# A subtraction of each normalized row tile, moved from VectorE to GpSimd, in the stage that finishes a graph attention layer

## The chip, the cores and the metric

The kernel runs on one core of a Trainium2 chip. The core's engines are TensorE (PE; its weight loads are PEld), VectorE (DVE), ScalarE (ACT), GpSimd (POOL) and SyncE (SP), each with an instruction queue of its own; they meet through semaphores. The metric is the device time of one execution in microseconds (us), lower is better. Before the change three timed runs gave 4061.72, 4068.97 and 4071.57 us, median 4068.97 us.

## What is computed

A graph network on 3125 nodes with 1024 features and 50000 edges: a layer norm and relu, a graph attention layer (GAT, 4 heads of 256), a residual sum, a second layer norm and relu, and two SAGE layers with a last residual sum. Cut to what matters here:

```python
h = jnp.maximum(_layernorm(x, axis=-1), 0.0)
x = x + relu(segment_sum(xp[src] * alpha[:, :, None], dst) + bias)   # attention layer, xp = h @ W
h = jnp.maximum(_layernorm(x, axis=-1), 0.0)
x = x + sage(relu(sage(h, W_self0, W_neigh0, b0)), W_self1, W_neigh1, b1)
```

`_layernorm` is `(x - mean) / sqrt(var + 1e-5)` along the row. The stage that the change touches begins when the sums over the edges are in SBUF and makes the second and third of these lines, up to the normalized h.

## The kernel before

The kernel is a sequence of stages with a barrier between them: tables of edges, a first normalization, the product with the attention weights, the sum over edges of the attention layer (`aggregate("gagg", ...)`), the finish of that layer (`gat_finish`, lines 1590 to 1716), and then twice a sum over edges and a product for the SAGE layers. All SAGE matmuls use f16 pairs: a row value v, scaled up, is kept as a high part, v rounded to f16, and a low part, v minus the high part, again in f16. A row of `h_rows` in DRAM is 1024 high parts, 1024 low parts and one scale.

`gat_finish` goes through 25 tiles of 125 rows by 1024 columns, with two slots for each buffer (slot = tile number modulo 2). For tile m:

- SyncE (`load`, L1621 to L1624) loads x and xp of the tile, in four DMAs, once x1 of tile m - 2 is ready.
- VectorE (`values`) computes four pieces of 256 columns at L1668 (own term plus edge sum), four at L1673 (division and bias), the relu and residual at L1676 (this gives x1, semaphore x1_ready at L1677), the row statistics at L1679 and L1682, and at L1683 the variance plus epsilon.
- ScalarE takes the root (L1704).
- VectorE (`normalize`) inverts it (L1690) and makes the shift (L1691).
- ScalarE computes the normalized, clipped row twice (L1713): h_sb in f32 and the first half of h16 in f16; then it counts up h_ready.
- VectorE (`split`, L1697) subtracts the f16 half from the f32 row and writes the result, in f16, to the second half of h16; it counts up lo_done.
- GpSimd stores x1 (`store_x1`, L1632) when x1_ready says so and h16 (`store_h`, L1636) when lo_done says so.

The order on each engine is written by `each_tile` (L136 to L152): straight code for tiles 0 and 1, then a loop of 11 turns with two tiles each, then straight code for the last ones. In its steady part it runs, on each engine, the `ahead1` step of tile m and then the `last` step of tile m - 1. So VectorE's order is values(m), normalize(m), split(m - 1), and GpSimd's is store_x1(m), store_h(m - 1). In the prologue values(0), normalize(0), values(1), normalize(1) follow each other with no split between; tile 2 is the first of the loop, and each even tile from 4 to 22 comes behind the loop's back edge. Tile 24 and the last two `last` steps come behind the loop. Inside the loop the tile number is a register, so that addresses of tile m and the values waited for are computed by the engine's queue ahead of the instruction that needs them; line 119 is the wait of the helper `chain`, by which VectorE waits for its own results.

Backward dependences: ScalarE writes h_sb and h16 of tile m only when lo_done covers tile m - 2 and the h store of tile m - 2 has landed; VectorE writes val of tile m only when the x1 store of tile m - 2 has landed and h_ready covers tile m - 2.

## Time and profile before

| | us |
|---|---|
| median of the three timed runs | 4068.97 |
| lowest, highest | 4061.72, 4071.57 |
| the profiled execution, own time | 4053.89 |
| its span, first to last instruction | 4052.2 |

The page of the profile gives busy time and share of the span by engine, and the span in 40 slices of 101 us, each digit a busy share in tenths. PEclk is the granted TensorE clock, in tenths of full speed; GB/s is what the DMA engines moved.

```profile
PE 3058.3 (75%) x20638; PEld 1746.6 (43%) x20638; DVE 2648.9 (65%) x4534; ACT 1150.8 (28%) x2637; POOL 1657.4 (41%) x1788
PE   0567878388888882007999999699668999997899
DVE  5646878688888887866555555555466555656443
POOL 4002222366666662114555555400145555555000
PEclk9978999699999996558999999899889999999999
```

The stage in question is slices 16 to 18 (counted from 1), where the PE row falls to 2, 0, 0. The profile numbers busy time only; register, branch and semaphore instructions of a queue are not in it, but can be asked for by line.

### The profile page before, as it was taken

How to read it: one execution, taken by the hardware profiler on the slowest of the kernel's cores; microseconds unless marked ns; L12 is line 12 of the kernel's file. 1: busy time of each engine (PE TensorE's matmuls, PEld its weight loads, DVE VectorE, ACT ScalarE, POOL GpSimd, SP SyncE). 2: the span in 40 equal slices, each digit the busy share in tenths (PEclk: the TensorE clock that was granted, in tenths of full speed). 3: DMA queues.
4: the chain of work that ended last, by engine and by line, in shares of the span. 5: the costliest groups of instructions: out<-in, count | busy, mean ns of one | idle time of the engine just before them, and what ended most of it. 6: DMA issues, size and time to landing. Idle time of an engine off the chain costs nothing. (4 is left out here: it accounts for less than half of the span.)

```text
span 4052.2 us, 74821 instructions
## 1 busy us (share of the span) xinstructions
PE 3058.3 (75%) x20638; PEld 1746.6 (43%) x20638; DVE 2648.9 (65%) x4534; ACT 1150.8 (28%) x2637; POOL 1657.4 (41%) x1788
## 2 busy tenths in 40 slices
PE   0567878388888882007999999699668999997899
PEld 0334544277777772003444444244324444442444
DVE  5646878688888887866555555555466555656443
ACT  3542343377777673310000000033200000000211
POOL 4002222366666662114555555400145555555000
PEclk9978999699999996558999999899889999999999
DMA  1456895388888885776999999622479999997333
GB/s 67 148 179 231 292 335 188 110 275 267 265 274 272 260 274 179 234 239 224 314 299 300 313 307 296 220 91 91 139 225 315 307 313 309 324 320 260 118 91 85
DMA packets 289524, 947.22 MB, mean 234 GB/s; under 512 B 57746, under 2 KB 58746, under 8 KB 289440
## 3 DMA queue, kind: packets, MB, share of 16 engines
q0 software_dynamic: 224912, 726.88, 53.8%
q1 hardware_dynamic: 64528, 219.29, 17.5%
q8 instruction: 45, 0.74, 0.1%
q14 instruction: 39, 0.32, 0.0%
HBM read 905.65 MB, written 130.59 MB: 256 GB/s over the span
## 5 line engine op out<-in xcount | busy, mean ns | idle before, releaser
L1434 POOL DMA_INDIRECT agg_got<-h_rows,agg_idx_now x896 | 898.0, 1002 | 654.3 <-issue 371.0
L1571 PE MATMUL agg_sum_ps<-agg_got,agg_hot 128*128 128x512 f16 x3584 | 878.1, 388 | 205.3 <-DVE agg_hot L1464 172.3
L1492 DVE TENSOR_TENSOR sum_acc<-agg_sum_ps,sum_acc 125x1024 f32 x448 | 548.7, 1225 | 434.4 <-PE agg_sum_ps L1571 322.9
L1555 PE MATMUL gagg_sum_ps<-gagg_got,gagg_hot_hi 128*128 128x256 f16 x3584 | 603.9, 274 | 198.6 <-DVE sums_acc L1492 129.3
L1571 PEld LDWEIGHTS agg_sum_ps<-agg_got,agg_hot 128*128 128x128 bf16 x3584 | 343.3, 99 | 664.0 <-DVE agg_hot L1464 216.9
L1530 ACT ACTIVATE gagg_hot_hi<-gagg_hot,gat_high_e 128x128 f16<-128x128 f16 x1792 | 547.7, 388 | 277.5 <-DVE gagg_hot L1459 229.2
L1434 POOL DMA_INDIRECT gagg_got<-xs_rows,gagg_idx_now x448 | 500.8, 1118 | 266.3 <-PE gagg_extra_ps L1560 120.5
L925 PE MATMUL agg_out_ps<-agg_w,agg_a_t 128*128 128x512 f16 x2400 | 577.3, 384 | 0.0
L818 PE MATMUL neigh_out_ps<-neigh_w,neigh_a_t 128*128 128x512 f16 x2400 | 529.3, 381 | 5.0 <-DMA neigh_w<-split_w 5.0
L1555 PE MATMUL gagg_sum_ps<-gagg_got,gagg_hot_lo 128*128 128x256 f16 x1792 | 490.5, 274 | 0.5 <-issue 0.4
L905 ACT ACTIVATE agg_a_t<-agg_turn_ps 128x2048 f16<-128x2048 f16 x50 | 93.8, 1877 | 1376.7 <-PE agg_turn_ps L913 1343.9
L1555 PEld LDWEIGHTS gagg_sum_ps<-gagg_got,gagg_hot_hi 128*128 128x128 f16 x3584 | 336.0, 98 | 249.1 <-issue 188.2
L1464 DVE TENSOR_SCALAR agg_hot<-all_iota_tn,all_rel,agg_got 128x128 bf16<-128x128 f32 x896 | 291.5, 361 | 228.9 <-DMA agg_got<-h_rows,agg_idx_now 143.7
L925 PEld LDWEIGHTS agg_out_ps<-agg_w,agg_a_t 128*128 128x128 f16 x2400 | 237.4, 99 | 297.6 <-issue 21.9
L818 PEld LDWEIGHTS neigh_out_ps<-neigh_w,neigh_a_t 128*128 128x128 f16 x2400 | 233.6, 98 | 279.8 <-DMA neigh_w<-split_w 5.3
L1470 DVE TENSOR_TENSOR gagg_hot_lo<-gagg_hot,gat_weight_e 128x512 f16<-128x512 f16 x448 | 290.1, 689 | 4.8
L913 PE MATMUL agg_turn_ps<-all_ident,agg_a 128*128 128x128 f16 x800 | 54.4, 223 | 292.2 <-DMA agg_a<-h_rows 292.2
L1492 DVE TENSOR_TENSOR sums_acc<-gagg_sum_ps,sums_acc 125x1024 f32 x224 | 274.1, 1224 | 0.0
L1335 PE MATMUL edg_out_ps<-gatw_w,edg_a_t 128*128 128x512 f16 x1008 | 254.0, 396 | 12.0 <-ACT edg_rows L1132 12.0
L1555 PEld LDWEIGHTS gagg_sum_ps<-gagg_got,gagg_hot_lo 128*128 128x128 f16 x1792 | 175.6, 98 | 22.3 <-issue 0.8
L913 PEld LDWEIGHTS agg_turn_ps<-all_ident,agg_a 128*128 128x128 f16 x800 | 50.2, 100 | 304.3 <-issue 292.8
L776 DVE SCALAR_TENSOR_TENSOR neigh_rows<-neigh_out_ps,neigh_post,neigh_rows 125x1024 f32<-125x1024 f32 x50 | 64.2, 1284 | 178.9 <-PE neigh_out_ps L818 178.9
(257 smaller groups left out, 2952.4 us busy)
## 6 DMA issues: line engine op xcount, KB each, us to landing
edg_piece<-slot_rows POOLq DMA_DIRECT2D x56, 512.0 KB
agg_a<-h_rows SPq DMA_DIRECT2D x50, 448.4 KB
part_rows<-agg_rows SPq DMA_DIRECT2D x50, 448.0 KB
neigh_rows<-part_rows SPq DMA_DIRECT2D x50, 448.0 KB
edg_w_buf<-in_L_gnn_W_self_dram SPq DMA_DIRECT2D x32, 512.0 KB
edg_w_buf<-in_L_gnn_W_neigh_dram SPq DMA_DIRECT2D x32, 512.0 KB
split_w<-edg_w_out SPq DMA_DIRECT2D x32, 512.0 KB, 7.8
agg_got<-h_rows,agg_idx_now POOLq DMA_INDIRECT x896
```

The costliest lines, as they stand in the source:

```text
L818: last = t.matmul(o, l, r, start=start, stop=stop)
L905: a.activation(a_t[:, :], turn_ps[:, :], ACT.Copy).then_inc(row_moved, 1)
L913: last = t.transpose(turn_ps[:, half, k, :], a16[:, half * D + k * P:half * D + (k + 1) * P], ident16[:, :])
L925: last = t.matmul(o, l, r, start=first, stop=final)
L1335: last = t.matmul(o, l, r, start=start, stop=stop)
L1434: g.indirect_dma_start(out=got[:, k, :], out_offset=None, in_=rows_in[:, :], in_offset=bass.IndirectOffsetOnAxis(ap=idx_now[:, s, k:k + 1] ...
L1464: v.tensor_scalar(hot[:, u % HOTS, :], iota_tn[:, :], rel[:, ds(s, 1)], got[:, u % R, 2 * D:ROW].bitcast(f32), ALU.is_equal, ALU.mult).the ...
L1470: v.tensor_tensor(hot_lo[:, u % HOTS, :, :], hot[:, u % HOTS:u % HOTS + 1, :].to_broadcast([P, H, P]), weight_e[:, ds(s, 1), 1, 0:H].rearr ...
L1492: v.tensor_tensor(acc[:, tl, :], sum_ps[n % 2][0:TN, :].rearrange("p (a d) -> p a d", a=1), acc[:, tl, :], ALU.add).then_inc(added, 1)
L1530: last = a.activation(hot_hi[:, u % HOTS, h, :], hot[:, u % HOTS, :], ACT.Copy, scale=high_e[:, ds(s, 1), h])
L1555: t.matmul(sum_ps[n % 2][:, h * C:(h + 1) * C], hot_k[:, u % HOTS, h, :], got[:, u % R, part * D + h * C:part * D + (h + 1) * C], start=(u ...
L1571: last = t.matmul(sum_ps[n % 2][:, q * HALF:(q + 1) * HALF], hot[:, u % HOTS, :], got[:, u % R, cols], start=(u == steps[0] and part == 0) ...
```

## The change

In `store_h` GpSimd now waits for h_ready itself and does the subtraction, on the same tile and slot and into the same place, before it waits for lo_done and issues the store. VectorE's `split` is gone, and with it its wait for h_ready; nothing takes its place in VectorE's order. The operation has the same shape (125 partitions by 1024 elements), inputs (f32 and f16) and output (f16). lo_done is now counted up by GpSimd.

```diff
                     def store_h(n, slot, half):
+                        g.wait_ge(h_ready, n + 1)
+                        g.tensor_tensor(h16[0:TN, slot, D:2 * D], h_sb[:, slot, :], h16[0:TN, slot, 0:D], ALU.subtract).then_inc(lo_done, 1)
                         g.wait_ge(lo_done, n + 1)
                         g.dma_start(tiles(h_rows)[:, ds(n, 1), :], h16[:, slot:slot + 1, :]).then_inc(stored_h[slot], 16)
...
-                    def split(n, slot, half):
-                        v.wait_ge(h_ready, n + 1)
-                        v.tensor_tensor(h16[:, slot, D:2 * D], h_sb[:, slot, :], h16[:, slot, 0:D], ALU.subtract).then_inc(lo_done, 1)
-                    each_tile(v, nothing, both(values, normalize), split)
+                    each_tile(v, nothing, both(values, normalize), nothing)
```

## Rows read from the trace of the kernel before

**Rows 1.** Table of stretches, the stage and one tile: start:end, length, engines, PEclk, DMA.

```profile
1565.00:1795.00 230.00, 0.00 (x0) 0.00 (x0) 193.41 (x400) 64.37 (x75) 26.20 (x50) 0.50 0.70 216
1650.96:1659.69 8.73, 0.00 (x0) 0.00 (x0) 7.73 (x18) 2.55 (x4) 1.04 (x2) 0.50 0.75 242
```

**Rows 2.** Timeline of steady tile 10: start us, us, engine, line, operation, idle before.

```profile
1650.96 1.66 DVE L1668 SCALAR_TENSOR_TENSOR fin_val<-fin_xp_sb,fin_own_n,sums_acc 125x256 f32<-125x256 f32 x4
1654.45 1.23 DVE L1676 SCALAR_TENSOR_TENSOR fin_val<-fin_val,fin_x_sb 125x1024 f32<-125x1024 f32 x1
1656.41 0.52 POOL L1632 DMA_DIRECT2D x_rows<-fin_val  x1 [4.19 <-DVEq L1677]
1657.26 0.21 DVE L1682 BATCH_NORM_AGGREGATE fin_mv<-fin_stats 125x2 f32<-125x12 f32 x1
1657.51 0.15 DVE L1683 TENSOR_SCALAR fin_mv<-fin_mv 125x1 f32<-125x1 f32 x1
1658.19 0.21 DVE L1691 TENSOR_SCALAR fin_shift<-fin_mv,fin_rstd 125x1 f32<-125x1 f32 x1
1658.55 1.23 DVE L1697 TENSOR_TENSOR fin_h<-fin_h_sb,fin_h 125x1024 f16<-125x1024 f32 x1
1659.69 0.48 DVE L1668 SCALAR_TENSOR_TENSOR fin_val<-fin_xp_sb,fin_own_n,sums_acc 125x256 f32<-125x256 f32 x1
```

**Rows 3.** Timeline, tiles 0 to 2, in straight code and into the loop.

```profile
1572.07 0.21 DVE L1691 TENSOR_SCALAR fin_shift<-fin_mv,fin_rstd 125x1 f32<-125x1 f32 x1
1572.43 1.67 DVE L1668 SCALAR_TENSOR_TENSOR fin_val<-fin_xp_sb,fin_own_n,sums_acc 125x256 f32<-125x256 f32 x4
1575.85 1.22 DVE L1676 SCALAR_TENSOR_TENSOR fin_val<-fin_val,fin_x_sb 125x1024 f32<-125x1024 f32 x1
1577.43 0.55 POOL L1632 DMA_DIRECT2D x_rows<-fin_val  x1 [6.92 <-DVEq L1677]
1581.08 1.67 DVE L1668 SCALAR_TENSOR_TENSOR fin_val<-fin_xp_sb,fin_own_n,sums_acc 125x256 f32<-125x256 f32 x4
```

**Rows 4.** Timeline, the last tile, number 24.

```profile
1773.26 1.66 DVE L1668 SCALAR_TENSOR_TENSOR fin_val<-fin_xp_sb,fin_own_n,sums_acc 125x256 f32<-125x256 f32 x4
1781.84 1.23 ACT L1713 ACTIVATE fin_h<-fin_val,fin_shift,fin_rstd 125x1024 f16<-125x1024 f32 x1
1784.61 0.52 POOL L1636 DMA_DIRECT2D h_rows<-fin_h  x1 [1.83 <-DVE fin_h L1697]
```

**Rows 5.** VectorE's queue by line: into tiles 10, 11 and 2.

```profile
L145 DVEq COMPARE_BRANCH  x1: 56/56/56, 1649.9 to 1649.9; - x1
L1668 DVEq FUSED_REGOPS  x2: 99/102/105, 1650.5 to 1650.8; - x2
...
L1663 DVEq EVENT_SEMAPHORE  x1: 50/50/50, 1658.6 to 1658.6; - x1
L1668 DVEq FUSED_REGOPS  x2: 99/102/105, 1658.7 to 1658.9; - x2
...
L1668 DVEq FUSED_REGOPS  x2: 124/126/129, 1580.4 to 1580.6; - x2
```

**Rows 6.** GpSimd's subtraction L1086 by its line: count, min/median/max ns.

```profile
L1086 POOL TENSOR_TENSOR edg_parts<-edg_rows,edg_parts x21: 2115/2134/5433, 317.6 to 724.2; 125x1024 f16<-125x1024 f32 x21
```

**Rows 7.** Timeline of GpSimd and VectorE in an earlier stage.

```profile
592.77 0.95 POOL L1084 DMA_DIRECT2D xp_rows<-edg_rows  x1 [11.08 <-ACT edg_rows L1132]
593.74 2.51 POOL L1086 TENSOR_TENSOR edg_parts<-edg_rows,edg_parts 125x1024 f16<-125x1024 f32 x1
...
653.35 2.53 POOL L1086 TENSOR_TENSOR edg_parts<-edg_rows,edg_parts 125x1024 f16<-125x1024 f32 x1 [0.35 <-ACT edg_parts L1136]
653.82 2.61 DVE L1250 TENSOR_TENSOR edg_anew<-gat_key_r 112x511 f32<-112x511 f32 x1
```

**Rows 8.** Timeline, the kernel's first stage.

```profile
56.01 2.37 POOL L304 TENSOR_TENSOR tab_tmp<-tab_w_sb,tab_att_sb 128x1024 f32<-128x1024 f32 x1
57.23 0.15 DVE L352 TENSOR_SCALAR tab_part_max<-tab_part_max 128x1 f32<-128x1 f32 x1
```

## The prediction

> **What bounds the kernel now.** I read the page's time slices first, then the table of stretches, then the timeline of one steady tile, and last the queues' own records. The stage that the change touches is one stretch of 230 us of the 4052.2 us span, in which TensorE does nothing, VectorE is busy 193 us of 230, ScalarE 64 and GpSimd 26 [rows 1]; the stretches to both sides of it belong to matmul stages that the change leaves alone. In one steady tile of 8.73 us VectorE is busy 7.73 us and the DMA engines 0.75 of the time [rows 1]. So VectorE sets the pace, and its chain is serial: L1668, L1673, L1676, the statistics, the root on ScalarE, L1690, L1691, the subtraction L1697 of the tile before, and then L1668 of the next tile [rows 2]. Neither L1668 nor L1697 shows a wait for a DMA there. Tile 2 starts at 1581.08 and tile 24 at 1773.26 [rows 3, 4]: 192.18 us for 22 periods, 8.735 us each. Nothing else runs in the stage, so what this period loses or gains, the kernel loses or gains.
>
> I count inside a tile from the start of its L1668 (1650.96 for tile 10): L1676 ends at +4.72, the x1 store's issue L1632 runs from +5.45 to +5.97, L1682 starts at +6.30, L1683 runs from +6.55 to +6.70, L1691 from +7.23 to +7.44, L1697 starts at +7.59, the next L1668 at +8.73 [rows 2].
>
> **What goes from VectorE.** L1697, 1.23 us long, stands between L1691 and the next L1668; from its start to that of L1668 are 1.14 us [rows 2]. Where the code has no subtraction there, between tiles 0 and 1, L1668 starts 0.15 us after L1691 ends (1572.28 to 1572.43) [rows 3]. Read from the engine alone the period would fall from 8.73 to 7.59, 1.14 us per tile. But that pair of tiles lies in straight code, and the steady ones in a loop, where the same queue must compute register values (addresses of tile m, values to wait for) before it can issue L1668. Today L1697 hides that. The records of the queue show it [rows 5]:
> - Inside the loop's body (tile 10 to 11; 11 such periods, the odd tiles 3 to 23): L1691 ends at 1658.40, the queue's semaphore step stands at 1658.6, and two register steps of 0.1 us, at 1658.7 and 1658.9, end at about 1658.98. L1668 could start 0.05 us later.
> - Across the back edge (into tile 10; 10 such periods, tiles 4 to 22): L1691 of tile 9 ends at 1649.66 (1650.96 - 8.74 + 7.44), then come a branch at 1649.9 and register steps until 1650.9; L1668 starts at 1650.96 now, when the engine is free, and could hardly have started earlier.
>
> The wait and the issue of L1697 go too. They cost between nothing and the 0.15 us that lie between L1691 and L1697; I take 0.09. Then L1668 starts at 1658.94 in place of 1659.69 in the one case (+7.98, call it 8.0), and at 1650.87 in place of 1650.96 in the other (a period of 8.64). At the loop's entry the register steps end at 1580.76 [rows 5], so tile 2 starts about 0.3 us earlier than at 1581.08.
>
> **What comes to GpSimd.** It waits for h of tile n, which is there by +9.81 of its own tile [rows 4], so in the first two microseconds of the next, subtracts, waits for its own result and issues the store. In its queue the new instruction stands behind the x1 store of tile n+1 (L1632), so it starts when that issue is done, at +5.97. The same instruction form (125x1024, f16 from f32) exists as L1086: 2115 ns at best, 2134 in the median, 5433 at worst [rows 6]. From a DMA issue to it there were 0.02 us (593.72 to 593.74) [rows 7]; I take 0.05. Its waiting value needs a register step, which should run while the DMA is being issued; if not, the price is the 0.36 us by which L1632 in the loop starts later after L1676 than in straight code (0.73 against 0.36) [rows 2, 3]. So the subtraction runs from +6.02 to +8.15, at worst to +8.51. GpSimd then has 0.52 us of issue left and is free long before the next +5.45.
>
> **What the two engines do to each other.** At 653.35 GpSimd's L1086 ran until 655.88; VectorE's L1250, with two inputs from SBUF and 511 elements, started at 653.82 and took 2.61 us, to 656.43, which is 0.55 us after GpSimd's end [rows 7]. That is a full block: such an instruction streams its elements (512 in about 0.53 us by that row) only when GpSimd is done. L1668 has two inputs from SBUF, 256 elements: it would end 0.29 us after GpSimd does, at +8.44. Unblocked it takes 0.48 us, so this is the same as a start at +7.96. The register steps allow +7.98 anyway. The block therefore costs nothing in the 11 odd periods and in the 10 even ones; with the late start of GpSimd it would be +8.32 in the odd ones. During the rest of the subtraction VectorE has only one-input work (L1679, which has started before) and instructions on one to twelve elements; I take these as not blocked, since L352, a one-element TENSOR_SCALAR, took its 0.15 us at 57.23 in the midst of a GpSimd TENSOR_TENSOR that ran from 56.01 to 58.38 [rows 8].
>
> The Trainium skill, "SBUF — State Buffer", section "Who interferes with whom", says that the ports are an exclusive lock and that whoever comes second blocks fully; by that rule, L1250 agrees. The same section says that copies, casts and tensor_scalar can take both ports and then contend with GpSimd. By that, L1683 and L1691 would be blocked, which is the third rival below; L352 does not bear it out.
>
> **DMA.** Loads and stores stay the same; only the h store of tile n moves, from 0.7 us after L1697's end, some +0.8 of tile n+1, to the end of GpSimd's subtraction plus 0.7, some +8.8 of tile n+1. ScalarE needs its buffer again for tile n+2 from about +7.5 of that tile, 6.7 us later. In a period the DMA engines have 0.75 x 8.73 = 6.5 us of work [rows 1], under 8.0, and the loads and the x1 store of the tile are ahead of it. If it came late, ScalarE would, but what it writes is wanted only at +6.0 of the tile after, 3.5 us after it is done. I cost the move at nothing; without this cover a period could not be shorter than the 6.5 us of DMA work plus the wait, which no case here reaches.
>
> **The sum.** 11 odd periods x (8.735 - 8.0) = 8.1 us; 10 even ones x 0.09 = 0.9; the entry 0.3; the exit of the loop into tile 24, in straight code and bound by the block at 7.96, 0.8. Against it the end: ScalarE ends the last tile at +9.81 (1783.07 - 1773.26), and the last h store is issued at +11.35 [rows 4]. With GpSimd it is 9.81 + 0.1 + 2.13 + 0.29 = 12.33, so 1.0 us more. Gain 8.1 + 0.9 + 0.3 + 0.8 - 1.0 = 9.1 us. Against the profiled execution's own 4053.89 us that gives 4044.8. That execution lies 15 us under the median of the three timed runs (4061.72 to 4071.57), so against the median 4068.97 it is 4059.9 us.
>
> **Rivals.**
> 1. The forecast, a gain of 5 to 10 us: 5 if GpSimd starts 0.36 us late (11 x 0.42 + 10 x 0.09 + 0.3 + 0.4 - 1.0 = 5.2), 10 if L1697's issue costs 0.15 and the odd periods are 7.96 (11 x 0.775 + 10 x 0.15 + 0.4 + 0.8 - 1.0 = 10.2). Chance 0.68.
> 2. The queue is not what holds L1668: register steps run earlier once L1697 is gone, and only the block counts. Then all 21 loop periods are 7.96: 21 x 0.775 + 1.15 (entry, 8.65 to 7.50) + 0.8 - 1.0 = 17.2 us, 4051.8 us. Against it: in both kinds of tile the steps stand behind L1691 [rows 5], whose result the queue waits for. Chance 0.08.
> 3. Slower: GpSimd holds the ports against VectorE's short instructions. L1683 at +6.55 then ends at 8.17, and what follows (root, L1690, L1691, register steps: 7.98 - 6.70 = 1.28 us to an odd L1668, 8.64 - 6.70 = 1.94 to an even one) gives periods of 9.45 and 10.1: 11 x 0.72 + 10 x 1.38 + about 1.4 for entry and exit + 1.0 = 24 us more, 4093 us. If L1682, at +6.30, is held, 29 us. It decides as soon as one instruction ahead of L1691 is held for over 0.7 us. For it: L1250; against it: L352. Chance 0.12.
> 4. Only L1691, which reads a second operand from SBUF, is held: it ends at 8.17 in place of 7.44. Odd periods stay at 8.7, even ones become 8.17 + 1.21 = 9.37, 6.4 us more; with the end's 1.0 and 0.2 won at the exit 7.2 us more, 4076.2 us. Chance 0.12.
>
> That the change does nothing is no case: GpSimd's own semaphore step replaces VectorE's one for one.
>
> **How the numbers follow.** The likeliest is the forecast, 4059.9 us; its own range is 4059 to 4064. A measurement of this kernel can tell about 0.3%, 12.2 us, from no change. Faster by that: rival 2 with 0.08, and 0.12 of the forecast's 0.68, where the scatter of the runs (10 us between the three) carries a gain of 9 over the bound; 0.20. Slower: rival 3, 0.12. The rest, 0.68, is within. The range takes in rivals 2 and 4 and leaves out 3: 4050 to 4077.
>
> **What would show it.** In the profile after: L1668 of odd tiles 8.0 us after the one before, of even ones 8.6; GpSimd's subtraction from about +6.0 for 2.13 us; L1668's first instruction up to 0.5 us long and no longer; L1682, L1683, L1691 at 0.21, 0.15, 0.21 us as now. If even periods fall to 8.0 too, the step on the register work is wrong; if a short instruction takes 1 us or more, the one on the block is.

## The result, and the profile after

| | before | after |
|---|---|---|
| median of five timed runs, us | 4068.97 | 4045.79 |
| lowest to highest, us | 4061.72 to 4071.57 | 4036.73 to 4055.86 |
| span of the profiled execution, us | 4052.2 | 4049.7 |
| the stage, from tile 0's first L1668 (L1670 after) to the next stage's first load, us | 229.7 | 217.8 |

The ratio of after to before is 0.9949, 95% interval 0.9928 to 0.9970: 23 us faster by the medians (12 to 29 by the interval), where 9.1 had been forecast, and 4 us below the predicted range. Both profiled executions stand off their medians, before's by 15 us to the fast side and after's (4051.37 us) by 5.6 us to the slow side, so the two spans say nothing of the gain; the stage lengths do. Ahead of the stage, where both kernels run the same code, the second profile took 10.7 us more (1575.7 against 1564.9 us). The stage gives 11.8 us. The other 11 us of the medians are not in the stage.

The page after the change: the engines' totals begin with TensorE's, then the busy tenths in 40 slices and the granted clock.

```profile
PE 3049.1 (75%) x20638; PEld 1740.6 (43%) x20638; DVE 2620.4 (65%) x4509; ACT 1150.9 (28%) x2637; POOL 1708.6 (42%) x1813
PE   0557878388888883007999999699669988997899
DVE  5546868688888887856555555555465565656443
POOL 4002222366666663334555555400045655555000
PEclk9978989699999997558999999899889999999999
```

The GpSimd row shows the move: its slices 16 to 18 were 2, 1, 1 and are now 3, 3, 3. The table of stretches, over the same 230 us as in [rows 1] and over the period of the same tile, number 10 (columns as there):

```profile
1565.00:1795.00 230.00, 0.00 (x0) 0.00 (x0) 167.05 (x383) 65.66 (x76) 78.54 (x75) 0.51 0.76 225
1656.95:1664.82 7.87, 0.00 (x0) 0.00 (x0) 6.59 (x16) 1.91 (x4) 2.94 (x3) 0.50 0.78 272
```

VectorE went from 193 to 167 us of the 230 and GpSimd from 26 to 79. The timeline of that period (start us, us, engine, line, operation, idle before and who ended it). The new lines of VectorE are two higher than before: L1670 was L1668, and L1684, L1685 and L1693 were L1682, L1683 and L1691. ScalarE's L1712 was L1713:

```profile
1656.95 1.67 DVE L1670 SCALAR_TENSOR_TENSOR fin_val<-fin_xp_sb,fin_own_n,sums_acc 125x256 f32<-125x256 f32 x4 [1.07 <-issue]
...
1662.41 0.52 POOL L1632 DMA_DIRECT2D x_rows<-fin_val  x1 [4.66 <-DVEq L1679]
1662.94 2.01 POOL L1636 TENSOR_TENSOR fin_h<-fin_h_sb,fin_h 125x1024 f16<-125x1024 f32 x1
1663.27 0.21 DVE L1684 BATCH_NORM_AGGREGATE fin_mv<-fin_stats 125x2 f32<-125x12 f32 x1
1663.51 0.15 DVE L1685 TENSOR_SCALAR fin_mv<-fin_mv 125x1 f32<-125x1 f32 x1
1664.19 0.21 DVE L1693 TENSOR_SCALAR fin_shift<-fin_mv,fin_rstd 125x1 f32<-125x1 f32 x1
1664.82 1.67 DVE L1670 SCALAR_TENSOR_TENSOR fin_val<-fin_xp_sb,fin_own_n,sums_acc 125x256 f32<-125x256 f32 x4 [0.42 <-DVE fin_shift L1693]
1665.62 0.54 POOL L1638 DMA_DIRECT2D h_rows<-fin_h  x1 [0.67 <-POOL fin_h L1636]
```

L1670 starts at 1656.95 and again at 1664.82, 7.87 us later, where there were 8.73 [rows 2]. GpSimd's subtraction L1636 starts 0.01 us after the x1 store's issue L1632 has ended, 5.99 us into the tile, and runs 2.01 us beside VectorE's short instructions, which take 0.21, 0.15 and 0.21 us as in [rows 2]. L1670 starts 0.13 us before it is done. Over the stage, by line (busy us, mean ns, idle before):

```profile
L1636 POOL TENSOR_TENSOR fin_h<-fin_h_sb,fin_h 125x1024 f16<-125x1024 f32 x25 | 51.8, 2072 | 1.8 <-ACT fin_h L1712 1.5
L1670 DVE SCALAR_TENSOR_TENSOR fin_val<-fin_xp_sb,fin_own_n,sums_acc 125x256 f32<-125x256 f32 x100 | 41.8, 480 | 23.9 <-issue 10.8 <-DMA fin_xp_sb<-xp_rows 7.2 <-DVE fin_shift L1693 5.8
```

The subtraction takes 2072 ns on GpSimd and took 1225 ns on VectorE; it alternates between 2.01 and 2.13 us by slot. The end of the stage, where the move costs something:

```profile
1771.01 1.72 DVE L1670 SCALAR_TENSOR_TENSOR fin_val<-fin_xp_sb,fin_own_n,sums_acc 125x256 f32<-125x256 f32 x4 [0.42 <-DVE fin_shift L1693]
1780.96 2.12 POOL L1636 TENSOR_TENSOR fin_h<-fin_h_sb,fin_h 125x1024 f16<-125x1024 f32 x1 [1.52 <-ACT fin_h L1712]
1783.38 0.54 POOL L1638 DMA_DIRECT2D h_rows<-fin_h  x1 [0.30 <-POOL fin_h L1636]
1793.52 0.41 SPq L844 DMA_DIRECT2D agg_w<-split_w  x1
```

The last h store is issued 12.37 us after the last tile's L1670 began; it was 11.35 [rows 4]. The next stage's first load (L844) follows at 22.51 us after that L1670, against 21.35 in before. The four pieces of this last tile take 1.72 us and not 1.67: the first one started at 1771.01, GpSimd's subtraction ran until 1771.26, and the piece ended 0.29 us after that, at 1771.55. Here, and in no other tile of the changed kernel, the block shows.

### The profile page after: what moved, and what is told of

Same layout as the page of the kernel before. It is cut to its first block and busy times, and to the rows that moved or that the text cites. A ratio compares the mean times of both kernels' runs of the same rounds, so it can differ in the third digit from the quotient of the medians.

```text
span 4049.7 us, 74821 instructions
## 1 busy us (share of the span) xinstructions
PE 3049.1 (75%) x20638; PEld 1740.6 (43%) x20638; DVE 2620.4 (65%) x4509; ACT 1150.9 (28%) x2637; POOL 1708.6 (42%) x1813
## 5 line engine op out<-in xcount | busy, mean ns | idle before, releaser
L1434 POOL DMA_INDIRECT agg_got<-h_rows,agg_idx_now x896 | 895.5, 999 | 648.7 <-issue 321.1
L1492 DVE TENSOR_TENSOR sum_acc<-agg_sum_ps,sum_acc 125x1024 f32 x448 | 548.4, 1224 | 413.4 <-PE agg_sum_ps L1571 313.5
L1434 POOL DMA_INDIRECT gagg_got<-xs_rows,gagg_idx_now x448 | 498.2, 1112 | 272.7 <-PE gagg_extra_ps L1560 158.0
L1464 DVE TENSOR_SCALAR agg_hot<-all_iota_tn,all_rel,agg_got 128x128 bf16<-128x128 f32 x896 | 292.5, 355 | 248.9 <-DMA agg_got<-h_rows,agg_idx_now 158.7
L1492 DVE TENSOR_TENSOR sums_acc<-gagg_sum_ps,sums_acc 125x1024 f32 x224 | 273.9, 1223 | 0.0
```

The lines of the kernel that those rows point to most:

```text
L1434: g.indirect_dma_start(out=got[:, k, :], out_offset=None, in_=rows_in[:, :], in_offset=bass.IndirectOffsetOnAxis(ap=idx_now[:, s, k:k + 1] ...
L1464: v.tensor_scalar(hot[:, u % HOTS, :], iota_tn[:, :], rel[:, ds(s, 1)], got[:, u % R, 2 * D:ROW].bitcast(f32), ALU.is_equal, ALU.mult).the ...
L1492: v.tensor_tensor(acc[:, tl, :], sum_ps[n % 2][0:TN, :].rearrange("p (a d) -> p a d", a=1), acc[:, tl, :], ALU.add).then_inc(added, 1)
```

## Experiments

Every kernel was timed in five rounds (the one with a second subtraction in three) beside runs of the kernel before on the same chip, and its ratio is to those. "The stage" is measured as in the table above.

**The same two kernels again, and the loops written out.** VectorE's program for the stage is a loop over pairs of tiles. In two kernels it is straight code (the loop's body, repeated), in a third GpSimd's as well.

```diff
-                    each_tile(v, nothing, both(values, normalize), split)
+                    each_tile_flat(v, nothing, both(values, normalize), split)   # before, VectorE straight
-                    each_tile(v, nothing, both(values, normalize), nothing)
+                    each_tile_flat(v, nothing, both(values, normalize), nothing) # after, VectorE straight
-                    each_tile(g, nothing, store_x1, store_h)
+                    each_tile_flat(g, nothing, store_x1, store_h)                # after, GpSimd straight too
```

Before again: 

> The kernel before, unchanged, timed against itself. The change won 23 us in the median of the runs, while its stage is 11.8 us shorter in the trace. Theory S (the rest is scatter of the other stages from execution to execution): the ratio here is 1.000 with an interval some 0.2% to each side, and the stretch ahead of the stage (1564.9 us before, 1575.7 after the change) differs from trace to trace by about 10 us with no edit at all. Theory R (the rest is real): this kernel's times lie within 3 us of each other, and the stretch ahead of the stage is again 1565 us.

After again: 

> The changed kernel, once more. Theory S: 12 us (0.3%) faster than before, the shortening of the stage from its first L1668 to the next stage's first load, 229.7 to 217.9 us. Theory R: again about 23 us (0.5%) faster. Periods in the stage 7.86 and 8.53 us, as in the first trace, under both.

Before, VectorE straight: 

> The kernel before with VectorE's loop in the stage written out as straight code: the control of the register steps. Before the change VectorE's subtraction lay over them, so straight code should bring nearly nothing: periods 8.65 us, as tile 1 to 2, in place of 8.735, the stage 2 us shorter, 0.9995. If register steps held the kernel before as well, more.

After, VectorE straight: 

> The changed kernel, with VectorE's loop in the stage written out as straight code (GpSimd, ScalarE and SyncE keep theirs), so that its queue has no register steps ahead of the first instruction of a tile. Theory Q (register steps set the periods of 7.86 and 8.53, and the block by GpSimd is real but hidden): all periods are equal, and now GpSimd's subtraction decides: it ends at about +8.03 of a tile, the next tile's first instruction then ends at +8.32, so the period is 7.84; that instruction shows up to 0.8 us in place of 0.48. The stage gets 7 us shorter, 4 to 5 us by 7.84 against 8.53 in 10 periods and a little at the entry. Without the block (rival): 7.50 in all, 15 us shorter. If register steps are not what holds the even tiles (rival): 7.86 and 8.53 stay.

After, both straight: 

> As the one before, and GpSimd's loop straight too, so that its store of x1 is issued 0.36 us earlier and the subtraction starts and ends 0.36 us earlier (+5.55 to +7.68 of a tile). Theory Q with the block: the subtraction now ends early enough for the next tile's first instruction (needed by +7.69), periods 7.50, the stage 15 us shorter than after the change. Without the block: 7.50 too, and equal to the run with VectorE's loop alone straight. A rival bound, the DMA engines, with 6.5 us of work per tile, would show as a wait for xp ahead of the first instruction of a tile and a period over 7.5.

| kernel | period of a tile, us | stage, us | ratio (interval) |
|---|---|---|---|
| before again | 8.73 | 229.6 | 1.0002 (0.9993 to 1.0011) |
| after again | 7.86 odd, 8.52 even | 217.5 | 0.9951 (0.9935 to 0.9966) |
| before, VectorE straight | 8.64 | 227.5 | 0.9991 (0.9979 to 1.0003) |
| after, VectorE straight | 7.72 and 7.83 in turn | 208.1 | 0.9933 (0.9917 to 0.9949) |
| after, both straight | 7.60 | 204.1 | 0.9928 (0.9915 to 0.9942) |

Before again stands at 1.0002, with 1562.5 us ahead of the stage; after again repeats the whole gain, with 1565.2 us there. So the 10.7 us by which the first two profiles differ ahead of the stage do not come with the change, and the gain outside the stage does.

Even tiles lie behind the loop's back edge, odd ones inside the body. The gap at the back edge vanishes in straight code (8.52 to 7.8 with the change, and only 8.73 to 8.64 without it). So the queue's steps at the back edge hold L1668, and L1697 covered most of them before: writing out VectorE's loop is worth 9.4 us of the stage with the change (13 with GpSimd's loop as well) and 2 without it. With VectorE alone straight, the period (expected: 7.84 in all tiles) is no longer the queue's but the block's:

```profile
1642.23 2.01 POOL L1652 TENSOR_TENSOR fin_h<-fin_h_sb,fin_h 125x1024 f16<-125x1024 f32 x1
1643.93 1.78 DVE L1686 SCALAR_TENSOR_TENSOR fin_val<-fin_xp_sb,fin_own_n,sums_acc 125x256 f32<-125x256 f32 x4 [0.25 <-DVE fin_shift L1709]
```

Four pieces at L1686 (L1670 in the looped kernel) take 1.78 us in place of 1.67. GpSimd's subtraction ends at 1644.24; the first piece starts at 1643.93, needs 0.48 us unblocked (1644.41) and, blocked until 1644.24, ends 0.29 us later at 1644.53. That is 0.12 us more, and 0.11 are seen. With GpSimd's program straight as well, the x1 store is issued 0.35 us behind L1694 (the relu and residual) in place of 0.73, the subtraction follows it, and the block is gone:

```profile
1639.90 2.13 POOL L1652 TENSOR_TENSOR fin_h<-fin_h_sb,fin_h 125x1024 f16<-125x1024 f32 x1
1641.52 0.21 DVE L1709 TENSOR_SCALAR fin_shift<-fin_mv,fin_rstd 125x1 f32<-125x1 f32 x1
1641.98 1.67 DVE L1686 SCALAR_TENSOR_TENSOR fin_val<-fin_xp_sb,fin_own_n,sums_acc 125x256 f32<-125x256 f32 x4 [0.25 <-DVE fin_shift L1709]
```

L1652 ends at 1642.03, the first piece starts at 1641.98 and the four take their 1.67. I had expected 7.50 here, as between tiles 0 and 1; 0.25 us lie between L1709's end and L1686 and not 0.15, so 7.60. This version has the lowest median of the study, 30 us under the kernel before (4020.81 us against 4050.91 on the same chip); in whole-kernel time it can't be told from the one with VectorE alone straight (4021.54).

**A second subtraction.** GpSimd does the subtraction twice, first into a buffer of its own that nobody reads.

```diff
                     def store_h(n, slot, half):
                         g.wait_ge(h_ready, n + 1)
+                        g.tensor_tensor(extra[:, :], h_sb[:, slot, :], h16[0:TN, slot, 0:D], ALU.subtract).then_inc(extra_done, 1)
                         g.tensor_tensor(h16[0:TN, slot, D:2 * D], h_sb[:, slot, :], h16[0:TN, slot, 0:D], ALU.subtract).then_inc(lo_done, 1)
+                        g.wait_ge(extra_done, n + 1)
```

> The changed kernel with a second, idle subtraction on GpSimd, into a buffer of its own, ahead of the real one: it doubles the suspected wait. GpSimd then works from +5.96 to +10.2 of a tile. Theory L (a GpSimd instruction that reads SBUF blocks a VectorE instruction with two SBUF inputs for its whole length, and two of them in a row block through): the next tile's first instruction ends at +10.5, all periods of the loop are 10.0 us, and the kernel is 30 us slower than before (1.0075). Rival (VectorE gets in between the two): it starts at +8.1, periods stay near 7.9 and 8.5, and the kernel is about as fast as with one subtraction. No block at all: the same 7.86 and 8.53.

Measured: ratio 1.0057 (1.0038 to 1.0076), stage 259.5 us, periods 9.3 and 10.4 to 10.5 where 10.0 had been expected in all. One tile of it, with the first of the four pieces at L1674 (L1670 in the changed kernel) alone:

```profile
1661.46 2.01 POOL L1638 TENSOR_TENSOR fin_extra<-fin_h_sb,fin_h 125x1024 f16<-125x1024 f32 x1
1661.77 0.21 DVE L1688 BATCH_NORM_AGGREGATE fin_mv<-fin_stats 125x2 f32<-125x12 f32 x1
1662.02 0.15 DVE L1689 TENSOR_SCALAR fin_mv<-fin_mv 125x1 f32<-125x1 f32 x1
1662.69 0.21 DVE L1697 TENSOR_SCALAR fin_shift<-fin_mv,fin_rstd 125x1 f32<-125x1 f32 x1
1663.32 2.38 DVE L1674 SCALAR_TENSOR_TENSOR fin_val<-fin_xp_sb,fin_own_n,sums_acc 125x256 f32<-125x256 f32 x1 [0.41 <-DVE fin_shift L1697]
1663.42 2.00 POOL L1639 TENSOR_TENSOR fin_h<-fin_h_sb,fin_h 125x1024 f16<-125x1024 f32 x1
```

GpSimd is in a subtraction from 1661.46 to 1663.47 and again from 1663.42 to 1665.42. The statistics' end L1688 and the short L1689 and L1697 run in the midst of the first at 0.21, 0.15 and 0.21 us: not held. The first piece begins at 1663.32, while the first subtraction still runs, and lasts 2.38 us in place of 0.48: it ends at 1665.71, 0.29 us after the second subtraction. So it waited through the end of the first and the whole of the second, and VectorE did not get in between. The three pieces behind it follow at their usual distance of 0.40 us, and all four take 3.57 us in place of 1.67. The expectation had the wait right and the period wrong: a tile is as long as in the changed kernel (7.86 or 8.53) plus what the pieces of the tile before were stretched, 1.48 us in even tiles (7.86 + 1.48 = 9.34) and 1.90 in odd ones (8.53 + 1.90 = 10.43). That is the block that the change keeps clear of, and the operations that it spares.

**The gain outside the stage.** In the profiles of after and after again one other stretch differed from before: the second sum over edges (`aggregate("agg1", ...)`), which the change does not touch. Candidates: the changed stage itself (theory R), scatter (theory S), or the place of the instructions that follow (theory P; theory PG for GpSimd's). The change takes five copies of the subtraction out of VectorE's program (tile 0, two in the loop's body, two behind it), so all of VectorE's later instructions stand five places further forward; the built programs have 2285 VectorE instructions before and 2280 after. Memsets of one element move them:

```diff
+                pad = sb("pad", [1, 16])
...
                     each_tile(v, nothing, both(values, normalize), split)   # nothing in place of split in after
+                    for k in range(11):                                     # or 5
+                        v.memset(pad[:, k:k + 1], 0.0)
```

Two controls: six such memsets at the end of GpSimd's program of the stage (the change lengthens that program by five, so six is one place more), and the eleven of VectorE behind the second sum over edges, where they shift nothing of it.

After, five memsets: 

> The changed kernel with five one-element memsets on VectorE behind the stage's last instruction, so that VectorE's code of the later stages lies again where it lay before the change. The change wins 20 us (interval 14 to 26), and the stage itself is 11.8 to 12.1 us shorter; in both traces of it the second sum over edges is 7 to 18 us shorter than in the two traces of before (819 and 827 against 834 and 838 us). Theory P (the place of VectorE's later code is what the rest comes from): 12 us faster than before (0.9970), second sum over edges 834 to 838 us. Theory S (rest is from elsewhere or scatter): as the changed kernel, 0.995, 819 to 827 us.

The same again: 

> The changed kernel with five one-element memsets on VectorE behind the stage, run again. Theory P (VectorE's later instructions stand where they stood in the kernel before, and this sets the second sum over edges): ratio 0.9961 as the first time (within 0.9948 and 0.9974) and that sum 831 to 838 us, with 6 or more drops of TensorE's granted clock, as in the four builds with before's VectorE code length. Theory S: that sum may as well come out at 819 to 829 us with 1 to 4 drops.

A third time, on another chip, beside after: 

> The changed kernel with five one-element memsets on VectorE behind the stage, which put its later instructions back where the kernel before had them. Theory P: 0.9965, that is, the stage's 12 us (0.9970) and next to nothing more; second sum over edges 825 us or longer with 8 or more clock drops. Theory S: 0.9955, within 2 us of the plain changed kernel.

After a fourth time, beside it: 

> The changed kernel once more, beside its padded form on the same chip. Theory P (the place of VectorE's later instructions gives the part outside the stage): ratio 0.9945, the mean of the last two, and at least 5 us faster than the padded form. Theory S (scatter): the two forms within 2 us of each other, both near 0.9955.

After a third time, beside the second of the runs with five: 

> The changed kernel once more. Two theories on the part of the gain that lies outside the stage. Theory R (the second sum over edges runs faster in every build whose stage after it differs from before by the change): ratio 0.995, within 0.9935 and 0.9966; the second sum over edges 819 to 829 us in the profile with 2 to 5 drops of TensorE's granted clock in it. Theory S (what that sum takes is scatter from one execution to the next, and the whole-kernel gain is the stage's 12 us): ratio 0.997, and a length anywhere between 819 and 839 us.

After, eleven: 

> The changed kernel with eleven one-element memsets on VectorE behind the stage, before the later stages' instructions (they add under 1 us of work and nothing uses them). Theory P (where VectorE's later instructions lie decides how the second sum over edges goes): the length of that sum moves with the number of memsets, so it may be near 820 or near 835 us, and the padding of five run again stays at 834. Theory S: no pattern by kernel; ratio 0.997 whatever the padding. Stage 217.5 us by both.

Before, eleven: 

> The kernel before with eleven one-element memsets on VectorE behind the stage; the stage itself is as in before (229.5 us). Theory P (the place of VectorE's later instructions sets the second sum over edges): if eleven shift them to a better place the ratio is 0.998 and the sum 820 to 829 us with few clock drops; if not, 1.000 and 831 us or more. Theory S: ratio 1.000 within 0.0015, and a length anywhere between 819 and 839 us. Theory R: ratio 1.000, and 831 us or more, since the stage is before's.

The same again: 

> The kernel before with eleven one-element memsets on VectorE behind the stage, run again. Theory P: ratio 0.996 again, within 0.9942 and 0.9978, with the stage at 229.7 us as in before and the gain in the sums over edges. Theory S: the first run's 0.996 was a draw, and this one gives 1.000 within 0.0015.

Before, five: 

> The kernel before with five such memsets instead of eleven. Theory P: another place of VectorE's later instructions, so a ratio of its own, anywhere from 0.995 to 1.001; by the runs of the changed kernel (its padding of five gave 0.9961 and 0.9963 against 0.9951 and 0.9939 without) five cost some 4 to 9 us against none there. Theory D (any addition behind the stage helps): 0.996 as with eleven. Theory S: 1.000 within 0.0015.

Before once more, beside the two above: 

> The kernel before once more, so that a trace of it stands beside the others on the same chip. Every theory: ratio 1.000 within 0.001. Theory P (the place of VectorE's later instructions sets how the second sum over edges goes): that sum about 15 us longer than in before_pad_v11_b of the same chip, with 8 to 10 drops of TensorE's granted clock against 3 to 5. Theory S (scatter from one execution to the next): no fixed order between the two.

Before, eleven behind the sum: 

> The kernel before with the eleven one-element memsets at the end of VectorE's program for the second sum over edges, so that the same work is added, and all instructions of both sums over edges that follow the stage stand where they stood. Theory P: ratio 1.000 within 0.0015. Theory D (adding them anywhere helps, whatever they shift): 0.996. Theory S: 1.000.

Before, six on GpSimd: 

> The kernel before with six one-element memsets on GpSimd behind the stage's last store, so that GpSimd's code of the later stages lies where it lies after the change. The stage itself stays 229.7 us. Theory PG (the place of GpSimd's later code brings the rest): about 8 us faster than before, 0.998, second sum over edges under 830 us. Otherwise 1.000, 834 to 838 us.

What they gave. Shift is how many places VectorE's later instructions stand behind where before has them. Pause is a reading of the timeline of the second sum, found by its result and not expected: the median of TensorE's waits of over 1.4 us for VectorE's L1464, without the first and last 90 us; there are 22 to 26, about one for each of the 25 rounds that carry a product. Low clock is how many of these are followed by a group of matmuls that ran at the lower clock (over 0.28 us each where 0.24 is usual); where a group is taken to begin moves some of these counts by one.

| kernel | shift | pause, us | low clock | second sum, us | ratio (interval) |
|---|---|---|---|---|---|
| before | 0 | 2.25 | 9 | 834.0 | |
| before again | 0 | 2.25 | 9 | 837.7 | 1.0002 (0.9993 to 1.0011) |
| before, third time | 0 | 2.25 | 9 | 827.6 | 0.9999 (0.9986 to 1.0012) |
| before, 6 on GpSimd | 0 | 2.25 | 6 | 831.0 | 0.9995 (0.9985 to 1.0006) |
| before, 11 behind the sum | 0 | 2.25 | 7 | 826.1 | 0.9996 (0.9986 to 1.0006) |
| after, 5 | 0 | 2.25 | 8 | 834.4 | 0.9961 (0.9948 to 0.9974) |
| after, 5, second time | 0 | 2.25 | 6 | 817.6 | 0.9963 (0.9950 to 0.9976) |
| after, 5, third time | 0 | 2.25 | 7 | 834.5 | 0.9977 (0.9965 to 0.9988) |
| before, 5 | +5 | 2.02 | 7 | 819.3 | 0.9980 (0.9970 to 0.9990) |
| after, 11 | +6 | 2.02 | 5 | 823.8 | 0.9957 (0.9941 to 0.9973) |
| before, 11 | +11 | 1.91 | 3 | 818.0 | 0.9960 (0.9942 to 0.9978) |
| before, 11, second time | +11 | 1.91 | 2 | 818.1 | 0.9979 (0.9966 to 0.9992) |
| after | -5 | 1.91 | 4 | 827.1 | 0.9949 (0.9928 to 0.9970) |
| after again | -5 | 1.91 | 2 | 819.2 | 0.9951 (0.9935 to 0.9966) |
| after, third time | -5 | 1.92 | 4 | 819.4 | 0.9939 (0.9921 to 0.9957) |
| after, fourth time | -5 | 1.92 | 3 | 824.4 | 0.9949 (0.9935 to 0.9964) |

The kernels with loops written out and with the second subtraction have pauses of 2.00 us in before with VectorE straight (838.6 us, 8 at low clock) and 1.91 in the three others (820.2, 824.9 and 828.9 us; 4, 2 and 1 at low clock), with shifts of +379, +354, +354 and -5.

Theory R falls: eleven memsets, with before's stage at 229.7 us, gave 0.9960 and 0.9979, both intervals below 1. That adding memsets anywhere helps (theory D) falls too: behind the sum they gave 0.9996, on GpSimd 0.9995. Nor is it the place of GpSimd's instructions: the three kernels after with five memsets have GpSimd's program as the change leaves it, and before's pause. Scatter alone falls by the pause, which follows the shift in all sixteen profiles and nothing else, and by the pair that ran on one chip: after 0.9949, after with its place restored 0.9977, 12 us apart. The place of VectorE's later instructions does it. Single expectations missed: before once more was to take about 15 us longer in that sum than before with eleven beside it and took 9.5 longer, and one profile speaks weakly against the theory: the second run of after with five was to take 831 to 838 us, has the 2.25 us pause and yet took only 817.6 us; that execution was the fastest of its seven (3934.34 us against a median of 3944.76), so a single profile's length scatters by some 10 us, and I rest nothing on one alone.

How the place becomes time shows at the boundary of a round, in the timelines of two kernels of the same call. Before (third time):

```profile
2964.58 1.22 DVE L899 TENSOR_TENSOR agg_rows<-agg_rows,agg_bias_sb 125x1024 f32<-125x1024 f32 x1
2965.23 1.45 POOL L1434 DMA_INDIRECT agg_got<-h_rows,agg_idx_now  x1 [0.93 <-PE agg_sum_ps L1571]
2966.14 0.57 DVE L1464 TENSOR_SCALAR agg_hot<-all_iota_tn,all_rel,agg_got 128x128 bf16<-128x128 f32 x1 [0.34 <-issue]
2966.77 1.48 PE L1571 MATMUL agg_sum_ps<-agg_got,agg_hot 128*128 128x512 f16 x6 [2.25 <-DVE agg_hot L1464]
```

Before with eleven memsets:

```profile
2963.84 1.23 DVE L899 TENSOR_TENSOR agg_rows<-agg_rows,agg_bias_sb 125x1024 f32<-125x1024 f32 x1
2964.51 1.44 POOL L1434 DMA_INDIRECT agg_got<-h_rows,agg_idx_now  x1 [0.93 <-PE agg_sum_ps L1571]
2965.29 0.34 DVE L1464 TENSOR_SCALAR agg_hot<-all_iota_tn,all_rel,agg_got 128x128 bf16<-128x128 f32 x1 [0.22 <-issue]
2965.69 1.92 PE L1571 MATMUL agg_sum_ps<-agg_got,agg_hot 128*128 128x512 f16 x8 [1.91 <-DVE agg_hot L1464]
```

VectorE ends L899, the last operation of the round, goes across its loop's back edge, and makes the next selection matrix (L1464), for which TensorE waits. From L899's end to L1464 are 0.34 us in the one and 0.22 in the other, and from there to TensorE's start 0.63 and 0.40. TensorE stood still for 2.25 and 1.91 us.

Both parts can be followed in the records of these traces (medians over rounds 4 to 22; steps are what the queue does itself). VectorE's queue has one gap there of about 0.13 to 0.17 us where 0.03 to 0.05 is usual, some 0.1 us too long, and it moves with the shift. In all eight kernels of shift 0 it lies between L192's register step and the next step, SEQ_ASSERT (0.134 us against 0.034 in all others), and L1464 waits for both. With a shift of -5 (after, four times, and the second subtraction) it lies exactly five instructions later, behind the start of the first L1464, and delays only the second one. With +5 it lies right ahead of L1492, the operation before the last two of the round, and with +6 one instruction ahead of that: it delays VectorE's chain while TensorE still has work. With before's straight code (+379) it lies right ahead of the first L1464, and with +11 and +354 nowhere between L1492 and TensorE's start. So some fixed places in the memory of VectorE's instructions cost 0.1 us when the queue passes them, and the shift decides which instruction stands there. In the first sum over edges none falls there in the seven kernels looked at (shifts 0, +5, +6, +11, -5, +354 and +379), and its pause is 2.00 to 2.02 us in all.

The other 0.23 us are the first L1464 itself, which takes 0.57 us in the one and 0.34 in the other. It depends on GpSimd, which issues an indirect DMA (L1434) at that time: in the 20 profiles together this L1464 took over 0.5 us in the 161 rounds in which such an issue was running and ended less than 0.574 us after L1464's start, and about 0.35 in the 223 in which it ended later and in the 96 in which none was running. The 0.11 us by which shift 0 starts L1464 later bring it into the first group. That GpSimd's issue holds the operation is the reading that fits; no run moved the issue by itself.

The second effect hangs on the pause. Stretches around a later boundary and the whole sum, before (third time) first (columns as in [rows 1], so the last three are PEclk, DMA share and GB/s), and below it the one with eleven memsets:

```profile
2992.00:2996.00 4.00, 1.49 (x8) 0.60 (x7) 2.74 (x5) 0.47 (x1) 2.77 (x3) 0.99 0.86 291
2996.00:3000.00 4.00, 4.00 (x13) 1.41 (x12) 3.32 (x7) 0.00 (x0) 2.00 (x3) 0.58 0.91 280
2827.30:3654.90 827.60, 702.29 (x3392) 315.43 (x3392) 497.24 (x750) 46.92 (x25) 466.85 (x504) 0.95 0.91 300
```

```profile
2992.00:2996.00 4.00, 2.09 (x11) 0.80 (x9) 3.13 (x5) 1.27 (x1) 2.76 (x4) 1.00 0.89 264
2996.00:3000.00 4.00, 4.00 (x21) 1.76 (x19) 3.53 (x7) 0.00 (x0) 2.53 (x3) 1.00 0.87 244
2827.90:3646.00 818.10, 691.06 (x3392) 310.95 (x3392) 501.60 (x750) 46.92 (x25) 467.12 (x504) 0.96 0.91 303
```

Right behind the pause (TensorE busy 1.49 of 4 us) before's granted clock averages 0.58 over 4 us, that is, mostly 1.2 in place of 2.4 GHz, and 13 matmuls run where the other kernel, busy 2.09 of 4 us there, runs 21 at full clock. Over the sum the same 3392 matmuls take 702 us of TensorE in the one and 691 in the other: 11 us more, where the sum is 9.5 us longer. That these falls come more often after the longer pause is seen in the table (6 to 9 against 2 to 4). It is no strict rule: two thirds of the 2.25 us pauses are followed by none, at 2.02 there are 5 and 7, and before with VectorE straight has 8 at 2.00.

The Trainium skill ("Runtime: NRT & Kernel Launch", section "Instruction fetch mechanics") says that a taken branch to code outside the pages at hand forces a fetch by DMA. The instruction queues' rows on the page would have to show more of them in the slower kernel:

```profile
q8 instruction: 45, 0.74, 0.1%
q14 instruction: 39, 0.32, 0.0%
```

These are of the kernel with eleven; before (third time) has the same 45 and 39, so by this rule nothing differs and the trace doesn't bear it out as the cause. The same skill ("Advanced Engine Details and Errata", section "Sequencer Memory") lists a sequencer cache with lines of 256 bytes; with 64 bytes for an instruction ("Vector Engine (DVE) Microarchitecture Reference", section "Instruction fetch and dispatch (NX sequencer)") a new line would begin with every fourth instruction. The traces do not bear that out as the cause either: the stretch from L1492 to TensorE's start holds some twenty instructions of VectorE and at most one long gap, and the shifts of -5 and +11, which are a multiple of four apart and gave the same pause, have the gap at different places. What begins at the places that cost 0.1 us stays open.

## Why the prediction was wrong

**What bounds the stage: right.** VectorE's chain sets the period, and it fell by what left that chain.

**Removed from VectorE: mechanism right, one reading wrong.** The forecast was 8.0 us for odd and 8.64 for even periods; measured are 7.86 and 8.52, and 8.15 from tile 1 to 2, where 8.35 was forecast. Two statements of the prediction failed: that L1668 "could hardly have started earlier" than it did behind the back edge (and in the body 0.05 us after 1658.98), and "The wait and the issue of L1697 go too. They cost between nothing and the 0.15 us that lie between L1691 and L1697; I take 0.09". VectorE's queue in after, into tile 10, up to the moment at which the first piece starts (1656.5 to 1656.97):

```profile
L1670 DVEq FUSED_REGOPS  x1: 105/105/105, 1656.7 to 1656.7; - x1
L1670 DVEq ALU_OP  x1: 45/45/45, 1656.9 to 1656.9; - x1
L1670 DVE SCALAR_TENSOR_TENSOR fin_val<-fin_xp_sb,fin_own_n,sums_acc x1: 484/484/484, 1657.0 to 1657.0; 125x256 f32<-125x256 f32 x1
```

Only one of the two FUSED_REGOPS of [rows 5] comes ahead of the piece. The second begins at 1656.98, when the piece has started (1656.955): it belongs to the second piece. The prediction took it (ending at 1650.90 and 1658.97 in before) for a condition of the first. In before the last step that the first piece needs ended at 1650.73 and 1658.80; in after the piece follows such a step by 0.05 and 0.06 us, so it could have started at 1650.78 and 1658.85, each time 0.18 us earlier than the prediction allowed. The issue of L1697 was taken too large: from the semaphore step behind L1691 to the queue's next step are 0.12 and 0.13 us with it and 0.08 and 0.09 without, so it cost 0.04 and not 0.09. Together 0.22 us come free where 0.09 stood: 8.735 - 0.22 = 8.52, and in the body 1658.85 - 0.04 - 1650.96 = 7.85, as measured within 0.01. By periods: 11 x (8.735 - 7.86) = 9.6 us in place of 8.1, 10 x (8.735 - 8.525) = 2.1 in place of 0.9, entry 0.5 in place of 0.3, exit (8.73 to 7.87) 0.9 in place of 0.8, together 13.1.

**That the queue's steps hold L1668, and not the block: right, but for tile 24.** Rival 2 needed 7.96 in all tiles; even ones stayed at 8.52, and straight code took the difference away.

**GpSimd's price and place: right.** Start at +5.99 (forecast +6.02), 2.01 to 2.13 us (2.13), its register step hidden beside the issue of L1632.

**The block: right in size, and narrower than the margin suggested.** The first L1670 piece is not stretched in the changed kernel; it starts 0.13 us before GpSimd's end in the period shown (1664.82 against 1664.95) and its 0.48 us hold a wait that short. In tile 24 it starts 0.24 us before GpSimd's end and is stretched by 0.05. Had the odd periods been 0.1 us shorter, the block would have shown, as it did with VectorE in straight code; a second subtraction, which the block did reach, made the stage 30 us longer than before's.

**Rivals 3 and 4: refuted.** L1684, L1685 and L1693 run under GpSimd's subtraction at unchanged durations in 24 of 24 tiles, in the changed kernel and under the doubled one. What I cited of the Trainium skill ("SBUF — State Buffer", section "Who interferes with whom") for rival 3, that a tensor_scalar can take both ports, did not happen for these one-column instructions (a tensor_scalar of 128 columns, L1464, did take 0.57 us in place of 0.35 beside GpSimd's DMA issue); for two-input VectorE operations the full block that the same section names is borne out.

**DMA moved at no cost: right in effect.** The h store did come late now and then: ScalarE waited for it twice in after (1.25 and 0.76 us; never in before), and 17 times with both loops straight, up to 2.6 us. The periods there stayed at 7.86 and 8.52, and at 7.60, so the cover that the prediction counted on was there and was used.

**The tail: right.** 12.37 us to the last store against 12.33; the next stage's first load came 1.16 us later, for 1.0 (0.9 in the second pair).

Sum of the stage: 13.0 us between the first and the last L1670 less 1.2 is 11.8, for 9.1. With the correct terms the forecast would have been 4057 us, within the predicted range and still 11 us above the result. What took the result out of the range is the next point.

**The step that failed most: "Nothing else runs in the stage, so what this period loses or gains, the kernel loses or gains."** This treated all other stages as fixed. Taking five instructions out of VectorE's program moved all that follow, and the second sum over edges, 25 rounds of it, ran with a pause of 1.91 us in place of 2.25: 0.34 x 25 = 8.5 us, and fewer falls of TensorE's clock on top, not all of which reaches the end (that sum keeps the DMA engines busy 0.91 of the time). That the pause got shorter and not longer was luck: nothing in the edit aimed at it. Measured on whole kernels, the four runs of after average 0.9947 and the three of after with the place restored 0.9967: 8 us. The latter is 13 us under before, which is the stage's 12. So of the 23 us, 12 are the move of the subtraction, about 8 the place of code that the change did not mean to touch, and the rest is within the interval of the measurement (8.5 us to each side).

## What to carry to other kernels

An instruction that is taken off a queue saves its duration only as far as nothing else of that queue was hidden behind it: look at the register, branch and semaphore records between its neighbours before counting the full time, settle which of them belong to the instruction that you count for and which to the one behind it, and write a short hot loop out if they come to the top. Before giving GpSimd an elementwise operation, lay its interval over VectorE's two-input operations; work on one to twelve columns passes beside it, while a one-input operation on 128 columns did take longer beside GpSimd's issue of an indirect DMA. And where a gain of half a per cent is at stake, shift the later code by a few idle instructions in both kernels: here eleven memsets that compute nothing were worth 0.2 to 0.4%, against 0.5% for the edit under study, of which 0.3% are its own.

## What the runs showed of the hardware

- Some places in the memory of VectorE's instructions cost its queue 0.10 to 0.12 us in passing (0.134 us in place of 0.034 between two steps). By which instruction stood there, at shifts of 0, +5 or +6, and -5 or +11 instructions, TensorE's wait in the second sum was 2.25, 2.02 or 1.91 us. The first of the two sums (`agg0`), with nearly the same code in another place, had 2.00 to 2.02 us in all these kernels.
- A one-input TENSOR_SCALAR of VectorE (128x128, f32 to bf16) took 0.57 us in place of 0.35 in the 161 of 480 rounds in which GpSimd's issue of an indirect DMA ended less than 0.574 us after its start.
- A two-input operation of VectorE that started under a GpSimd subtraction ended 0.29 us after it, whether it waited 0.05, 0.12 or 1.90 us for that, and two subtractions in a row held it as one. TENSOR_SCALAR, RECIPROCAL and BATCH_NORM_AGGREGATE on one to twelve columns kept 0.15 to 0.21 us under them.
- An instruction's issue cost VectorE's queue 0.04 us, a register step about 0.1 us.
- Behind a pause of about 2 us TensorE's granted clock fell to the lower of its two levels for a few us in 2 to 9 of about 25 cases, more often after 2.25 us than after 1.91.
- In this stage the back edge left VectorE idle for 1.07 us before L1670 against 0.42 inside the body and 0.25 in straight code.
- Chips differ by more than the change: the unchanged kernel took 4051 to 4069 us (medians) on some chips and 3958 on two others. 78 us of it lie in the attention layer's sum over edges (804.3 against 726.4 us in the profiles of before again and before, third time). VectorE's rows of one line there, first the slower chip's (idle before, and who ended it):

```profile
L1490 DVE TENSOR_TENSOR sums_acc_x<-gagg_extra_ps,sums_acc_x 125x9 f32 x224 | 37.4, 167 | 97.3 <-remote 87.6 <-PE gagg_extra_ps L1560 7.3 <-issue 1.8
```

```profile
L1490 DVE TENSOR_TENSOR sums_acc_x<-gagg_extra_ps,sums_acc_x 125x9 f32 x224 | 37.1, 165 | 28.4 <-PE gagg_extra_ps L1560 26.8 <-issue 0.2
```

The work takes as long on both. The idle time before it is 97 us on the one and 28 on the other, and 88 of the 97 the profile puts down to a semaphore event from elsewhere, of which the other shows none. What it is was not looked into, and ratios are taken within a chip for this reason.
